# Gated cross-attention and feed-forward: Q, K and V projected already turned, stacks put together by transfers in chip memory

## The reference

```python
x = x + tanh(g_xattn) * attention(layernorm(x), ctx, ctx)     # Wq 512x512, Wk and Wv 512x128, Wo 512x512, with biases
x = x + tanh(g_ffn) * ffn(layernorm(x))                       # w1, w3: 1792x512, w2: 512x1792, with 128x128 block scales
# attention: 32 query heads in 8 groups of 4 that share a key/value head, head size 16,
#   softmax(Q K^T / 4) V, then @ Wo + bo
# ffn: silu(x w1^T) * (x w3^T), then @ w2^T; the activation quantisation of the reference is undone in the same step
```

## Time and profile before

| | |
|---|---|
| median of 3 runs | 391.83 us (391.08 to 392.46) |
| the profiled execution's own time | 391.85 us |
| its span, first to last instruction | 390.1 us |
| PE busy | 377.4 us (97%), granted clock 1.00 |
| DVE busy | 271.7 us (70%) |
| ACT busy | 209.1 us (54%) |
| POOL busy | 160.5 us (41%) |
| DMA | 20.98 MB, 54 GB/s over the span |

### The profile page before, as it was taken

How to read it: one execution, slowest core, us unless ns; L and a number is a source line. 1 busy time by engine, 2 the same in 40 slices (tenths; PEclk the granted TensorE clock), 3 DMA queues, 4 the chain that set the end, 5 groups by cost and what they waited for, 6 DMA issues and landing times.

```text
span 390.1 us, 6293 instructions
## 1 busy us (share of the span) xinstructions
PE 377.4 (97%) x2350; PEld 307.5 (79%) x2350; DVE 271.7 (70%) x452; ACT 209.1 (54%) x367; POOL 160.5 (41%) x135
## 2 busy tenths in 40 slices
PE   7789999999998999999999999999999999999996
PEld 5578888888887677878888888888888888888885
DVE  5978998979998967898776777543954344554334
ACT  4678999998999986552332332332332332332320
POOL 6558889898999785264333443000000000000000
PEclk9999999999999999999999999999999999999999
DMA  8903104100000040295000000000200000000002
GB/s 289 342 14 86 32 2 167 46 40 6 2 6 3 3 166 2 86 416 227 0 0 0 0 0 0 0 0 2 108 0 0 0 0 0 0 0 0 0 0 108
DMA packets 6817, 20.98 MB, mean 54 GB/s; under 512 B 875, under 2 KB 1131, under 8 KB 6668
## 3 DMA queue, kind: packets, MB, share of 16 engines
q1 hardware_dynamic: 6364, 19.92, 14.0%
q10 hardware_dynamic: 432, 0.79, 0.5%
HBM read 18.28 MB, written 2.10 MB: 52 GB/s over the span
## 4 chain that ended last, share of the span: by engine, by line
PE 83%; DVE 9%; DMA 3%; SPq 2%; ACT 1%; issue 1%; POOL 0%; DVEq 0%
PE ps L1767 23%; PE ps L1769 23%; PE ps L1768 22%; PE ps L1819 3%; PE ps L1809 3%; PE ps L1774 3%; DMA gsc<-in_small 3%; DVE MX L1142 2%; PE ps L1827 2%; PE ps L1775 1%; PE ps L1828 1%; DVE x2HL L1172 1%; DVE X L1183 1%; DVE aTL L1153 1%; DMA Qst<-Mrow 1%
## 5 line engine op out<-in xcount | busy, mean ns | idle before, releaser
L1767 PE MATMUL ps<-x2HL,w13H 128*128 128x512 f32 x224 | 89.1, 398 | 0.0
L1769 PE MATMUL ps<-x2HL,w13L 128*128 128x512 f32 x224 | 88.6, 395 | 0.0
L1768 PE MATMUL ps<-x2HL,w13H 128*128 128x512 f32 x224 | 88.4, 395 | 0.0
L340 POOL TENSOR_TENSOR PL<-E,PH 128x512 f16<-128x512 f32 x64 | 74.1, 1174 | 13.2 <-ACT E L609 7.2
L351 POOL TENSOR_TENSOR wres<-wres,gsc 128x1536 f32<-128x1536 f32 x14 | 42.5, 3037 | 44.2 <-DVE hf L1196 44.2
L632 ACT ACTIVATE T<-ps 128x512 f32<-128x512 f32 x28 | 16.7, 597 | 79.0 <-PE ps L1769 79.0
L640 ACT ACTIVATE hH<-hf 128x512 fp32r<-128x512 f32 x28 | 17.7, 632 | 63.5 <-DVE hf L1196 63.5
L1769 PEld LDWEIGHTS ps<-x2HL,w13L 128*128 128x128 f32 x224 | 42.0, 187 | 10.4
L1768 PEld LDWEIGHTS ps<-x2HL,w13H 128*128 128x128 f32 x224 | 42.0, 188 | 9.8
L1189 DVE SCALAR_TENSOR_TENSOR A<-T,ps 128x512 f32<-128x512 f32 x28 | 19.2, 685 | 43.8 <-ACT T L632 43.8
L1767 PEld LDWEIGHTS ps<-x2HL,w13H 128*128 128x128 f32 x224 | 42.0, 188 | 9.5
(11 more groups left out here) (112 smaller groups left out, 712.8 us busy)
## 6 DMA issues: line engine op xcount, KB each, us to landing
wres<-in_wff SPq DMA_DIRECT2D x14, 768.0 KB, 6.7
X<-in_x SPq DMA_DIRECT2D x8, 256.0 KB, 11.1
ct<-in_ctxt SPq DMA_DIRECT2D x7, 256.0 KB, 3.2
raw<-in_wproj SPq DMA_DIRECT2D x3, 512.0 KB, 6.3
out<-X SPq DMA_DIRECT2D x6, 256.0 KB, 2.0
raw<-in_wproj SPq DMA_DIRECT2D x1, 1024.0 KB, 9.4
Qst<-Mrow SPq DMA_DIRECT2D x32, 8.0 KB
out<-X ACTq DMA_DIRECT2D x2, 256.0 KB, 2.1
```

Source lines behind the costliest of these rows:

```text
L340: pool.tensor_tensor(PL[:, g % NL, :], E[:, g % NE, :], PH[:, g, :], ALU.subtract).then_inc(pL_ok, 1)
L1767: pe.matmul(out_ap, aH, bH, start=start, stop=False)
L1768: pe.matmul(out_ap, aH, bL, start=False, stop=False)
L1769: return pe.matmul(out_ap, aL, bH, start=False, stop=stop)
```

## The change

Batches go through the projections in pairs, and Q, K and V come out with features on partitions and the 256 tokens of two batches as columns: the weights are now the matmul's first operand and the turned tokens the second.

- `project_q` makes one quarter j of Q (128 features: all eight key heads, query j of each group) for two batches, 12 matmuls of 256 columns; four quarters per pair. `project_kv` makes K and V separately, 12 matmuls of 256 columns each. The biases are now one number per partition and are added at the eviction (`q_high`, `k_high`, `v_bias`); the bias matmuls are gone, with the rows of ones.
- `stack_q`, `stack_k`, `q_stacked` and `k_stacked` are gone. High and low parts lie in `QTH`, `QTL`, `KTH`, `KTL`; SP copies them to their rows in `Qst` and `kst`: `queries_in` (three transfers of 32 partitions per batch and set of heads), `keys_in` (two transfers of 32 partitions and two of 16 per pair of batches and set of heads). All four quarters must be there before a batch's first `scores`.
- `max_in` is one transfer of 16 rows per batch, with the four sets' rows copied to each set; `select_rows` is one transfer per slot. `scores_t` runs over 112 rows instead of 100.
- V is turned back to tokens by two transposes per pair (`turn_v`), and its three parts are made in PSUM for two batches at once, two of the steps on ACT.
- `context_high` goes from POOL to ACT; `max_low` mostly from DVE to POOL; some residues, bias additions and high copies change engine; all instruction lists are written in a new order.
- Apart from the first three transfers on ACT (ctx of batches 0 and 1 and the bias; before it was one) and two stores at the end, SP issues every transfer, waiting for `kT_H`, `kT_L`, `qT_H`, `qT_L` (parts are there), `st_ps` (a slot's last reader is done) and `mrows`.

```diff
-            def stack_k(h, bank):
-            def stack_q(h, bank):
...
-            def project_kv(n, bank, k):
-                project(bank, 2 * KVD, ctH[:, n % 2], ctL[:, n % 2], KV0, k)
-
-            def add_bias(bank, width, b0):
-
-                return pe.matmul(bank[:, 0:width], ones[:], brow[:, b0:b0 + width], start=False, stop=True)
+            def project_kv(bank, w0, k0, k1):
+                for k in range(k0, k1):
+                    w = slice(w0 + k * KVD, w0 + (k + 1) * KVD)
+                    m = three(bank[:, 0:TWO], WpH[:, w], WpL[:, w], ctH[:, k, :, :], ctL[:, k, :, :], k == 0, k == KB - 1)
+                return m
+
+            def project_q(bank, j, k0, k1):
+                for k in range(k0, k1):
+                    c = Q0 + (j // 2) * KB * TWO + k * TWO + (j % 2) * P
+                    w = slice(c, c + P)
+                    m = three(bank[:, 0:TWO], WpH[:, w], WpL[:, w], xTH[:, k, :, :], xTL[:, k, :, :], k == 0, k == KB - 1)
+                return m
+
+            def turn_v(bank):
+                for b in range(2):
+                    m = turn(bank[:, b * P:(b + 1) * P], VT[:, b * P:(b + 1) * P])
+                return m
...
+        def keys_in(eng, n, h, low):
+            done = (k_in0, k_in1, k_in2, k_in3)[h]
+            s = (NBATCH - NKST + n % NKST) * P
+            if low:
+                for gg in range(2):
+                    r, a = 64 + 16 * gg, 32 * h + 16 * gg
+                    eng.dma_start(r32(x2HL[r:r + DH, gg, h, s:s + TWO]), r32(KTL[a:a + DH, gg, :])).then_inc(done, 16)
+            else:
+                for t in range(2):
+                    eng.dma_start(r32(x2HL[32 * t:32 * t + 32, :, h, s:s + TWO]),
+                                 r32(KTH[32 * h:32 * h + 32, :, :])).then_inc(done, 16)
+
+        def queries_in(eng, n, h, low):
+            done = ((q_in00, q_in01), (q_in10, q_in11), (q_in20, q_in21), (q_in30, q_in31))[h][n % 2]
+            for t in ((1,) if low else (0, 2)):
+                eng.dma_start(r32(Qst[32 * t:32 * t + 32, n % 2, h, :]),
+                             r32((QTL if low else QTH)[32 * h:32 * h + 32, n % 2, :, :])
+                             .rearrange("r j q -> r (j q)")).then_inc(done, 16)
+
+        def max_in(eng, n):
+            eng.dma_start(r32(Qst[ROWS:ROWS + NM, n % 2, :, :]),
+                         r32(Mrow[0:NM, :]).unsqueeze(1).broadcast_to([NM, PAIRS, GJ * P])).then_inc(mrow_in, 16)
...
+            def k_high(bank, gg):
+                act.wait_ge(sides, 2)
+                act.activation(KTH[:, gg, :], bank[:, 0:TWO], ACT.Identity, bias=bside[:, gg:gg + 1],
+                               scale=side[:, gg:gg + 1]).then_inc(kT_H, 1)
+            def q_high(bank, j):
+                act.wait_ge(bias_in, 16)
+                act.activation(QTH[:, :, j, :], bank[:, 0:TWO].rearrange("p (b q) -> p b q", b=2), ACT.Identity,
+                               bias=biasT[:, BQ + j:BQ + j + 1]).then_inc(qT_H, 1)
```

More of the change, by code:

```diff
@@ new lines, in _ @@
+            tokens_in(sp, 5)
+            sp.wait_ge(sel_ok, 3)
+            select_rows(sp, 1)
+            queries_in(sp, 1, 1, 1)
+            queries_in(sp, 1, 0, 0)
+            queries_in(sp, 1, 1, 0)
+            queries_in(sp, 1, 2, 0)
+            queries_in(sp, 1, 3, 0)
+            select_rows(sp, 2)
+            select_rows(sp, 0)
+            sp.wait_ge(mrows, 1)
+            max_in(sp, 0)
+            keys_in(sp, 2, 0, 1)
+            select_rows(sp, 3)
+            keys_in(sp, 2, 1, 0)
@@ new lines, in _ @@
+            sp.wait_ge(st_ps, 14)
+            queries_in(sp, 3, 2, 1)
+            queries_in(sp, 3, 2, 0)
+            sp.wait_ge(st_ps, 16)
+            queries_in(sp, 3, 3, 0)
+            weights_in(sp, 1)
+            sp.wait_ge(mrows, 3)
+            max_in(sp, 2)
+            queries_in(sp, 3, 3, 1)
+            keys_in(sp, 4, 2, 0)
+            keys_in(sp, 4, 1, 1)
+            keys_in(sp, 4, 0, 1)
+            keys_in(sp, 4, 2, 1)
+            keys_in(sp, 4, 0, 0)
+            keys_in(sp, 4, 3, 1)
@@ L555, in _ @@
             root2(5)
+            scale(2)
             pool.wait_ge(ve2_ok, 7)
@@ new lines, in _ @@
+            k_high(W1, 1)
+            weights_high(wo_in, O0, PW, woH_ok)
+            context_high(5)
+            act.wait_ge(vt_ps, 2)
+            v_first(2, W2)
+            act.wait_ge(r1_ok, 2)
+            v_second(2, W2)
+            act.wait_ge(mT_ps, 1)
+            max_rows(W2)
+            act.wait_ge(q_in11, 48)
+            act.wait_ge(q_in21, 48)
+            act.wait_ge(q_in31, 48)
+            q_high(W0, 0)
+            q_high(W1, 1)
+            act.wait_ge(nb1_ok, 5)
+            normalise(4)
@@ new lines, in _ @@
+            exp_full(7)
+            exp_half(6)
+            normalise(6)
+            exp_half(7)
+            act.wait_ge(q_in11, 96)
+            act.wait_ge(q_in21, 96)
+            act.wait_ge(q_in31, 96)
+            q_high(W2, 0)
+            act.wait_ge(st_ps, 17)
+            exp_half(0)
+            exp_full(0)
+            act.wait_ge(st_ps, 18)
+            exp_half(1)
+            q_high(W1, 1)
+            exp_full(1)
+            act.wait_ge(st_ps, 19)
+            exp_half(2)
+            act.wait_ge(pL_ok, 15)
@@ new lines, in _ @@
+            exp_full(2)
+            act.wait_ge(st_ps, 20)
+            exp_full(3)
+            exp_half(3)
+            act.wait_ge(q_ps, 11)
+            q_high(W2, 2)
+            act.wait_ge(st_ps, 21)
+            exp_half(4)
+            act.wait_ge(pL_ok, 17)
+            exp_full(4)
+            act.wait_ge(st_ps, 22)
+            exp_full(5)
+            o_high(W0)
+            act.wait_ge(mT_ps, 4)
+            max_rows(W2)
+            exp_half(5)
+            act.wait_ge(nb2_ok, 1)
@@ L1968, in _ @@
-            turn4(W1, xn).then_inc(xT_ps, 1)
-            pe.wait_ge(PH_ok, 3)
-            pe.wait_ge(mrow_in2, 16)
-            scores_t(0, 4)
-            stack_k(0, W2)
-            scores(1, 3)
-            pe.wait_ge(PH_ok, 4)
+            project_kv(W0, V0, 2, 4).then_inc(v_ps, 1)
+            project_kv(W2, K0, 0, 2)
+            pe.wait_ge(mL_ok, 1)
+            turn_max(W1)
+            pe.wait_ge(E_ok, 4)
             scores_t(0, 5)
-            pe.wait_ge(qtokL, 3)
-            stack_q(0, W0)
```

2537 lines of the change are left out of this document (1217 added, 1320 removed).

## The result

The changed kernel takes **415.50 us** (median of 4 runs, 412.58 to 419.78), the kernel before beside it 392.14 (391.08 to 392.50): a ratio of 1.058, 95% interval 1.051 to 1.064. One of the four (419.78) ran in a slower state, and the ratio leaves it out. The change makes the kernel slower by 23 us where 14 less were forecast; of the rivals, "SP becomes the bound, slower" (408 to 414) came nearest. The profiled execution took 416.25 us, with a span of 414.5 against 390.1.

What follows compares the result with a forecast made beforehand. The prediction took the sum of PE's instructions as the bound (83% of the span). 391.85 - 16.8 (PE) + 2 (start) + 1 (later pairs) = 378.05, said as 378; range 371 to 390, its own forecast 374 to 382.

Steps and rivals of the forecast that it cites:

- SP becomes the bound, slower: Rival: at 0.82 us an issue, a pair takes 35 us of SP against 31.3; 408 to 414, chance 0.11.
- SP then is busy 3/4 of the time and hides.: Attention pairs: 43 transfers at 0.48 us are 21 us of SP, hidden beside PE's pair of about 27.
- I take 0.48, since a query transfer is one run of 2 KB per partition: Price of one SP issue, taken near the 0.44 us row for a load of 128 partitions.
- eats the gain: Threshold: from 27/43 = 0.63 us an issue, SP's queue takes away the gain; slower only from 0.73.
- The rule of the Trainium skill: SP's transfers: DMA engines number the largest divisor of the outer dimension up to 16, so 32 or 16 partitions issue cheaply.
- +2 for the start: Start: first `scores` near 24 and `scores_t` near 36 us, partly won back; +2 us, bounds 0 and +7.
- +1 for the later pairs, bounds 0 and +10: Three later pairs: transfers run ahead of need, but `q_high` waits for landed queries and 768 KB loads share the queue.
- The tail: 0: End of attention: `weights_in(2)` and `scale(2)` come later but PE has 13 us of other matmuls; 0, without cover up to +3.
- The granted clock: Whole kernel: a clock below 1.00 anywhere was listed as a sign of being wrong that no term included.
- PE, removed and reshaped: -16.8: PE: stacks -15.8, bias matmuls -2.8, Q reshaped +0.9 at most, `turn_v` +0.9; sum -16.8 us.
- ACT -25, POOL -4, DVE somewhat lighter: Busy time of the other engines: ACT -25 us net, POOL -4, DVE lighter by some uncounted us; hidden beside PE.
- The landing, 2.29 us: Added wait for stacks: a transfer within chip memory took 2.29 us, against 0.6 for an eviction before.

Runs made afterwards that it cites:

- experiment 10: Changed kernel without the query transfers of batches 2 to 7, the key transfers of batches 4 to 7 and their waits: 396.95 us, ratio 1.016.
- experiment 2: Changed kernel with the first pair's queries of both batches in one transfer, 12 transfers fewer at the start, same bytes: 410.69 us, ratio 1.051.
- Experiment 8: Changed kernel with 40 extra transfers of no use issued by SP during the feed-forward, of various row counts and sources: 415.48 us.
- experiments 1 and 15: 26 warm-up matmuls instead of 14 on the changed kernel: 412.72 us; three times 5 matmuls on zeros ahead of PE's waits, on the second combination: 402.40 us.
- The second combination: Changed kernel with merged first-pair queries, 26 warm-up matmuls, weight loads behind `max_in(2)`, chunk 2 early, GpSimd scalings held back, x2 residues earlier: 400.79 us.

## Why the prediction was wrong

- **"SP then is busy 3/4 of the time and hides."** This step failed: the overlap, and below it the price. Without 104 of the 160 transfers the kernel is 18.5 us faster (experiment 10), and with 12 fewer issues in the first pair the first `scores_t` comes 5.6 us earlier (experiment 2). The average over a pair says little, because PE waits for single transfers at the end of each burst.
- **"I take 0.48, since a query transfer is one run of 2 KB per partition."** An issue takes 0.59 to 0.61 us with a distance of 0.64. The right row was in the earlier trace rows, 2.45/4 for `Mrow`; I had set it aside for the load from HBM, because of the 32 partitions. Experiment 8 shows that within chip memory partitions and row length do not matter. The dearest row, 6.58/8 = 0.82, hid nearly the same price: one of its eight issues took 1.61 us, one 0.81, and six 0.64 to 0.67. But by the forecast's own working the right price moves little: 43 x 0.64 = 27.5 us of SP against PE's 27 is 2 us over four pairs, and 26 x 0.16 = 4 more at the start, so some 384 and not 415. It brings SP to the threshold from which it "eats the gain" (0.63); the rest is the overlap.
- **The rule of the Trainium skill** (DMA: Bandwidth & Descriptors, "Why a DMA increments its semaphore by 16 and not by 1") on the number of engines was read as making 32 partitions cheap. Experiment 8 speaks against that reading for on-chip transfers: 0.60, 0.59, 0.59 and 0.61 us for 128, 32, 16 and 4 rows.
- **"+2 for the start"** was +14.5. The steps were right (four query parts first, keys, then 26 transfers ahead of `max_in`), but they were priced at 13 us and as overlapping: 16 key and 24 query transfers plus loads took SP from 15.2 to 44.3 us. Merging 12 of them gave 5.6 us back.
- **"+1 for the later pairs, bounds 0 and +10"**: idle time grew by 13.9 us up to batch 2 and 8.2 behind it. That the bound lay in bursts was missed: 43 issues per pair fit on average, but they come when the parts are ready, and PE waits at the end of each burst. About 5 us of this is the pair of big loads ahead of `max_in(2)`, which the text named ("loads of 768 KB stand in the same queue") without working it out.
- **"The tail: 0"** was +3.0, and for a reason not in the text. `weights_in(2)` did no harm; GpSimd's scalings of chunks 3 and 4 stood in the way of VectorE's residues in the kernel before too (1.72 and 2.04 us for two `h_low`, and a wait of 0.61 us on PE), and now they covered two residues ahead of the last two of x2.
- **The granted clock** was named as what none of the terms had. It was at 0.50, that is 1.2 GHz, in five stretches. Four began inside waits of PE of 3.09, 2.56, 4.89 and 3.92 us, the fifth 1.9 us behind one of 1.52. Where PE has nothing but work, the cost can be read: 12 matmuls of the first `y` run at 0.43 us instead of 0.23 until the clock is back at 196 us, about 2.5 us. In the others PE had work too (busy 6.1 of 6.7 us from 63.7 us on), but what they cost can't be told from the waits around them; experiments 1 and 15 gave no clear gain for removing one.
- **PE, removed and reshaped: -16.8.** The mechanism was right, and -14.6 by the estimate above.
- **ACT -25, POOL -4, DVE somewhat lighter.** Measured -15.8, -8.0 and -3.7 us busy. Evictions of 256 columns take 0.47 us (`QTH` and `VT`, with a bias per partition), 0.58 (`KTH`, with a bias and a scale) and 0.63 (the copies into `Vp`), not the 0.38 between the rows for 128 and 512. The scale vector is worth 0.10 of that; what the bias costs is not shown, since no run copies 256 columns in the same form without one. None of these engines held the kernel.
- **The landing, 2.29 us**, was right: 2.0 us for queries and keys, 3.2 for maxima (which are 128 KB now).
- **The rival** that came true, with a chance of 0.11, had the right mechanism and side, at 0.82 us an issue, and put the time at 408 to 414 against 415.5; that it came so near is partly luck. 0.64 was enough, since its threshold (0.73) assumed the issues spread evenly and the start overlapped.

What stays open: how much of the 10.7 us at the start could be won by another order of the first pair. The second combination still reaches its first `scores_t` 9.8 us later than the kernel before, and no run here took the projections of the second batch out of its way. Also open is why a load from HBM directly behind on-chip transfers took 0.58 to 1.47 us to issue in the changed kernel, and 0.44 to 0.49 in the kernel before.

## What to carry to other kernels

A transfer is not free because its bytes are few: count the issues per round, price each by a row with the same kind of source and destination, and compare the sum with the round both on average and in the burst ahead of the first consumer. Keep loads of hundreds of KB, in whichever queue, out of the 8 us ahead of a small transfer that an engine waits for. Handing issues to a second engine pays only where that engine has idle time at that very place.

## What was not expected of the hardware

- SP takes 0.59 to 0.61 us to issue a transfer within chip memory behind another one, whether it has 4 or 128 rows of 2 KB (or 32 or 128 of 512 bytes), and 0.42 to 0.43 for a load from HBM of 16 rows or more behind another load; ScalarE takes 0.60 to 0.62 for the same on-chip transfer.
- Behind two loads of 768 KB a transfer of 128 KB took 7.6, 8.0 and 7.7 us from issue to its reader's start in three kernels, and 3.3 to 3.4 without them. Transfers of 64 KB beside two such loads in ScalarE's queue took 5.4 to 6.2 us to land, and 2.0 before them.
- VectorE's subtraction of two on-chip operands took 2.51 and 3.24 us beside GpSimd's scalings and 0.68 without; with an operand in PSUM it was not slowed.
